# The second convolution of an audio tower as three fp32r products of high and low parts, with a shorter opening and weights loaded later

## What is computed

```python
h = x[:, None, :]                      # x: 64 x 4000
for w, g, b, s in zip(conv_ws, ln_gs, ln_bs, strides):   # (128,10,5), 4 x (128,3,2), 2 x (128,2,2)
    h = _conv1d(h, w, s)
    h = jnp.swapaxes(h, -2, -1)
    h = _fp32_layernorm(h, g, b)       # over the 128 channels
    h = jnp.swapaxes(h, -2, -1)
    h = jax.nn.gelu(h, approximate=False)
h = _fp32_layernorm(jnp.swapaxes(h, 1, 2), fln_g, fln_b) @ proj_w + proj_b    # 64 x 12 x 192
h = h + _L0_attn_ref(_layernorm(h), w_qkv, w_proj, b_proj)    # 12 heads, 64 landmarks, iterated inverse
h = h + _L0_ffn_ref(_layernorm(h), ...)                       # 8 experts, top 2, and a shared one
```

## Time and profile before

| | |
|---|---|
| median of 3 runs | 970.81 us (970.58 to 972.19) |
| the profiled execution | 965.42 us, span 963.7 us |
| PE busy | 711.2 us, 74% of the span, 3435 records |
| DVE busy | 631.7 us, 66%, 1471 instructions |
| ACT busy | 306.4 us, 32%, 505 instructions |
| products of L564, fp32 | 291.7 us, 720 records |
| copies of L724, 128x800 and smaller | 56.6 us, 58 instructions |
| squares of L625 | mean 0.86 us |
| mean granted clock of TensorE | 0.864 of full speed |

### The profile page before, as it was taken

The page is one execution under the profiler, slowest core; times in us unless marked ns, Lnnn a source line. Parts: engine busy times, 40 slices in busy tenths (PEclk is TensorE's granted clock), DMA queues, the critical chain, the costliest instruction groups (busy, mean ns, idle before and its releaser), DMA issues. The chain is left out here.

```text
span 963.7 us, 10716 instructions
## 1 busy us (share of the span) xinstructions
PE 711.2 (74%) x3435; PEld 511.1 (53%) x3435; DVE 631.7 (66%) x1471; ACT 306.4 (32%) x505; POOL 214.2 (22%) x253
## 2 busy tenths in 40 slices
PE   0069998999879997999897536544554446399987
PEld 0026664656545664566564325434554445399977
DVE  4918655774658555144645455899999999734377
ACT  0042345333432344332323121202333321136433
POOL 3000000000000000000000030655776679218401
PEclk9999998999979998899997557767777777879999
DMA  1350420024000410000000070000000000200000
GB/s 56 43 124 1 92 48 1 1 39 101 0 2 0 92 36 0 1 1 1 0 1 1 2 302 0 1 0 0 1 0 0 0 0 0 74 0 1 2 1 25
DMA packets 22553, 25.29 MB, mean 26 GB/s; under 512 B 17052, under 2 KB 21212, under 8 KB 21404
## 3 DMA queue, kind: packets, MB, share of 16 engines
q1 hardware_dynamic: 22508, 24.74, 10.5%
HBM read 21.05 MB, written 3.66 MB: 26 GB/s over the span
## 5 line engine op out<-in xcount | busy, mean ns | idle before, releaser
L564 PE MATMUL ps<-h,w 128*128 128x400 f32 x720 | 291.7, 549 | 1.9 <-ACT h L632 1.8
L564 PEld LDWEIGHTS ps<-h,w 128*128 128x128 f32 x720 | 139.6, 200 | 106.0 <-issue 103.3
L1055 PE MATMUL pt<-for_pe,ident 128*128 128x156 f32 (+2 forms) x420 | 98.4, 415 | 86.1 <-DVE for_pe L1248 86.1
L1055 PEld LDWEIGHTS pt<-for_pe,ident 128*128 128x128 f32 x420 | 90.3, 277 | 94.2 <-DVE for_pe L1248 90.2
L724 DVE COPY h<-ps 128x800 f32<-128x800 f32 (+2 forms) x58 | 56.6, 975 | 95.7 <-PE ps L564 95.0
L577 PEld LDWEIGHTS ps<-averager,sq 128*100 128x100 f32 (+2 forms) x1024 | 100.7, 173 | 22.9 <-ACT sq L625 18.6
L577 PE MATMUL ps<-averager,sq 128*100 128x1 f32 (+2 forms) x1024 | 101.2, 229 | 8.5 <-ACT sq L625 8.1
L625 ACT ACTIVATE sq<-h 128x800 f32<-128x800 f32 (+2 forms) x58 | 49.8, 858 | 177.9 <-DVE h L724 177.9
L632 ACT ACTIVATE h<-h,lnp 128x800 f32<-128x800 f32 (+2 forms) x58 | 60.5, 1042 | 83.1 <-DVE h L755 81.2
L755 DVE TENSOR_TENSOR h<-h,ps 128x400 f32<-128x400 f32 (+2 forms) x116 | 60.0, 559 | 38.2 <-PE ps L593 38.2
L604 ACT ACTIVATE h<-ps,lnp 128x800 f32<-128x800 f32 x64 | 63.4, 1010 | 63.5 <-PE ps L525 63.3
(11 more groups left out here) (268 smaller groups left out, 1032.2 us busy)
## 6 DMA issues: line engine op xcount, KB each, us to landing
late<-windows_dram SPq DMA_DIRECT2D x24, 375.0 KB, 7.4
gate_w<-in_gate_w SPq DMA_DIRECT2D x1, 3456.0 KB, 13.6
up_w<-in_up_w SPq DMA_DIRECT2D x1, 3456.0 KB, 19.1
windows_dram<-parts SPq DMA_DIRECT2D x12, 250.0 KB, 5.0
acts<-in_down_w SPq DMA_DIRECT2D x1, 1728.0 KB, 7.9
w<-in_w SPq DMA_DIRECT2D x1, 1024.0 KB, 6.2
xs<-in_x SPq DMA_DIRECT2D x4, 252.5 KB, 4.2
out_tokens<-hidden SPq DMA_DIRECT2D x6, 96.0 KB, 1.6
```

Source lines behind the costliest of these rows:

```text
L564: mm = pe.matmul(out, w[:, L.first_tap + t, :], source(l, s, 2 * p + c, t), start=(t == 0), stop=(t == L.taps - 1))
L1055: mm = pe.matmul(pt[:, job.bank + n, 0:wide], ident[:, :], sum_buffers[n][:, k * wide:(k + 1) * wide], start=(k == 0), stop=(k == job.term ...
```

## The change

The second convolution's fp32 products become fp32r products of parts. ScalarE rounds each batch of `h0` to fp32r (`rounded`, into `h0_hi`), VectorE takes what is left (`remainder`, into `h0_lo`); both have four places in turn (`TURNS`). The weights of layer 1 are split once. A batch then takes nine products: high by high, low weights by high, high weights by low, three taps each. `h0` is written with even and odd positions apart, so that each product reads 400 positions in a row. A new entry `split` in the plan is the rounding and the remainder of one batch; three of the next round's stand behind `conv(3, 1, 0)`. Round 0 gets a plan of its own: an opening of 3 first products in place of 9, and two instead of one in each of six steps of the section. `attention_weights` moves to the head of `expert_weights`, and the tiles that it fills are allotted there; some tiles of the tower's start share the space of later ones, which adds a wait for `w0_in` on VectorE.

```diff
 AHEAD = GROUP + 1
-POS0, ROW0 = 800, 802
+OPENING = 3
+POS0 = 800
+PLANE = POS0 // 2 + 1
+TURNS = 4
+SPLIT_AHEAD = 3
...
-def round_plan(last):
+def round_plan(last, opening=False):
...
+    waiting = list(range(OPENING if opening else AHEAD, ROUND))
+    soon = lambda: first(waiting.pop(0))
+    split = lambda *batches: [order.append(("split", int(b >= ROUND), b % ROUND // GROUP, b % GROUP)) for b in batches]
+    in_turn = lambda b: lambda: split(b)
+    catch_up = lambda: soon()() if opening else None
     prep(0, 2)
-    conv(1, 0, 0, first(9))
+    catch_up()
+    split(3)
+    conv(1, 0, 0, soon(), in_turn(4))
     prep(2, 4)
-    conv(1, 0, 1, first(10), var(1, 0, 0))
+    catch_up()
+    split(5)
+    conv(1, 0, 1, soon(), in_turn(6), var(1, 0, 0))
...
-    conv(1, 1, 1, first(14), rows(1, 0), var(1, 1, 0), scale(1, 0, 0, 1))
+    catch_up()
+    split(13)
+    conv(1, 1, 1, soon(), in_turn(14), rows(1, 0), var(1, 1, 0), scale(1, 0, 0, 1))
...
-    conv(1, 1, 2, first(15), var(1, 1, 1), scale(1, 0, 4, 5))
+    conv(1, 1, 2, soon(), in_turn(15), var(1, 1, 1), scale(1, 0, 4, 5))
+    assert not waiting
...
+        split(*range(ROUND, ROUND + SPLIT_AHEAD))
...
+    def __init__(self, rounds, per, ahead=AHEAD):
+        self.pair = ahead + per["pair"] * rounds
         self.conv, self.sets = per["conv"] * rounds, per["norm"] * rounds
+        self.split = SPLIT_AHEAD + ROUND * rounds
...
-        h0 = sb("h0", [P, 2, GROUP, ROW0])
+        h0 = sb("h0", [P, 2, GROUP, 2, POS0 // 2])
+        h0_hi, h0_lo = (sb(n, [P, TURNS, 2, PLANE], F32R) for n in ("h0_hi", "h0_lo"))
+        w1_hi, w1_lo = (sb(n, [P, L1.taps, CH], F32R) for n in ("w1_hi", "w1_lo"))
...
-        w0_parts = sb("w0_parts", [K0, PARTS, CH], BF16)
-        w0_rest = sb("w0_rest", [K0, CH])
...
-        w0_pairs = sb("w0_pairs", [P, K0, K0])
...
+        w0_parts = parts[0:K0, 0, :, :].rearrange("p k t -> p (k t)")[:, 0:PARTS * CH].rearrange("p (a c) -> p a c", a=PARTS)
...
+        w0_pairs = flat_u[:, 0:K0 * K0].rearrange("p (a b) -> p a b", a=K0)
+        w0_rest = flat_u[0:K0, K0 * K0:K0 * K0 + CH]
...
-            if batch >= AHEAD:
+            if plan is opening and batch < OPENING:
+                return batch + 1
+            if plan is opening or batch >= AHEAD:
                 return o.pair + number_of(plan, "first", 0, s, b, "pair") + 1
-            if isinstance(r, int) and r == 0:
-                return batch + 1
...
+        def wait_batch_read(eng, plan, r, o, batch):
+            if batch < 0:
+                if isinstance(r, int) and r == 0:
+                    return
+                b = batch + ROUND
+                pair, halves = o.pair - per["pair"] + number_of(body, "conv", 1, 1, b % GROUP // 2, "pair"), ROUND // 2 * (r - 1)
+            else:
+                b = batch
+                pair, halves = o.pair + number_of(plan, "conv", 1, b // GROUP, b % GROUP // 2, "pair"), ROUND // 2 * r
+            if b % 2:
+                eng.wait_ge(y_ready, pair + 1)
+            else:
+                eng.wait_ge(batch_read, halves + b // 2 + 1)
...
-                attention_weights(sp, io, res)
...
+                read_first = OPENING + number_of(opening, "first", 0, 0, GROUP - 1, "pair") + 1
...
-                    sp.wait_ge(y_ready, AHEAD + per["pair"] * (r - 1))
+                    sp.wait_ge(y_ready, max(AHEAD, read_first) + per["pair"] * (r - 1))
...
-                pool.memset(h0[:, :, :, POS0:ROW0], 0.0).then_inc(s_const, 1)
+                pool.memset(h0_hi[:, :, :, PLANE - 1:PLANE].bitcast(F32), 0.0).then_inc(s_const, 1)
+                pool.memset(h0_lo[:, :, :, PLANE - 1:PLANE].bitcast(F32), 0.0).then_inc(s_const, 1)
...
-                for b in range(AHEAD):
-                    if b % GROUP == 0:
-                        pe.wait_ge(win_in[b // GROUP], SLOT_IN)
+                pe.wait_ge(win_in[0], SLOT_IN)
+                for b in range(OPENING):
                     if b >= 2:
                         pe.wait_ge(y_taken, b - 1)
-                    first(b, (b + AHEAD) % 2)
+                    first(b, (b + OPENING) % 2)
...
-                            if l == 1 and p == 0:
-                                pe.wait_ge(win_in[s], SLOT_IN * (r + 2))
+                            if p == 0:
+                                pe.wait_ge(win_in[s], SLOT_IN * (r + l + 1))
...
-                                pe.wait_ge(y_taken, batch_taken(plan, r, o, GROUP * s + 2 * p + c))
+                                pe.wait_ge(lo_done, ROUND * r + GROUP * s + 2 * p + c + 1)
...
-                            for t in range(L.taps):
-                                mm = pe.matmul(out, w[:, L.first_tap + t, :], source(l, s, 2 * p + c, t),
-                                               start=(t == 0), stop=(t == L.taps - 1))
+                            if l == 1:
+                                hi, lo = h0_hi[:, (2 * p + c) % TURNS, :, :], h0_lo[:, (2 * p + c) % TURNS, :, :]
+                                products = [(a, b, t) for a, b in ((w1_hi, hi), (w1_lo, hi), (w1_hi, lo)) for t in range(L.taps)]
+                                for j, (a, b, t) in enumerate(products):
+                                    mm = pe.matmul(ypair[n["bank"]][:, c, 0:L.cols], a[:, t, :], b[:, t % 2, t // 2:t // 2 + L.pos],
+                                                   start=(j == 0), stop=(j == len(products) - 1))
+                                if not c:
+                                    mm.then_inc(batch_read, 1)
...
-                    act.activation(h0[:, s, p, 0:POS0].rearrange("p (h t) -> p h t", h=2), ypair[b][:, :, 0:400],
+                    act.activation(h0[:, s, p, :, :].rearrange("p q (h i) -> p q h i", h=2),
+                                   ypair[b][:, :, 0:POS0 // 2].rearrange("p h (i q) -> p q h i", q=2),
                                    ACT.Gelu, scale=lnp[:, 0:1], bias=lnp[:, 1:2]).then_inc(y_taken, 1)
 
+                def rounded(s, p):
+                    act.copy(h0_hi[:, p % TURNS, :, 0:POS0 // 2], h0[:, s, p, :, :]).then_inc(hi_done, 1)
...
-                for b in range(AHEAD):
-                    first(b // GROUP, b % GROUP, (b + AHEAD) % 2, b)
+                for b in range(OPENING):
+                    first(b // GROUP, b % GROUP, (b + OPENING) % 2, b)
+                for b in range(SPLIT_AHEAD):
+                    act.wait_ge(y_taken, b + 1)
+                    rounded(0, b)
...
+                        elif what == "split":
+                            act.wait_ge(y_taken, batch_taken(plan, r, o, GROUP * s + p, l))
+                            wait_batch_read(act, plan, r, o, ROUND * l + GROUP * s + p - TURNS)
+                            rounded(s, p)
...
-                        if not (isinstance(r, int) and r == 0):
+                        if isinstance(r, int) and r == 0:
+                            dve.wait_ge(w0_in, 16 * PARTS * PARTS)
+                        else:
...
+                dve.wait_ge(s_w0, 5)
...
-                nc.vector.nop(nofuse=True).then_inc(weights_ready, 1)
+                steps.done(nc.vector.tensor_copy(w1_hi[:, :, :], w[:, 0:L1.taps, :]))
+                steps.settle()
+                nc.vector.tensor_tensor(w1_lo[:, :, :], w[:, 0:L1.taps, :], w1_hi[:, :, :].bitcast(F32),
+                                        ALU.subtract).then_inc(weights_ready, 1)
...
+                def remainder(s, p):
+                    nc.vector.tensor_tensor(h0_lo[:, p % TURNS, :, 0:POS0 // 2], h0[:, s, p, :, :],
+                                            h0_hi[:, p % TURNS, :, 0:POS0 // 2].bitcast(F32), ALU.subtract).then_inc(lo_done, 1)
+                for b in range(SPLIT_AHEAD):
+                    dve.wait_ge(hi_done, b + 1)
+                    remainder(0, b)
...
+                        elif what == "split":
+                            dve.wait_ge(hi_done, o.split + n["split"] + 1)
+                            remainder(s, p)
...
-                run(body, 0, Origin(0, per))
+                run(opening, 0, Origin(0, per, OPENING))
...
-    return {"ident": sb("ident", [P, P]), "ident_b": sb("ident_b", [P, P], BF16),
-            "expert_pick": sb("expert_pick", [PICK_ROWS, PICK_TILES, P], BF16), "h6": sb("h6", [P, TOK]), "lnp": sb("lnp", [P, 16]),
-            "proj_w": sb("proj_w", [CH, D]), "qkv_w": sb("qkv_w", [96, KD, 3 * D]),
-            "out_w": sb("out_w", [96, KD, D]),
+    return {"ident": sb("ident", [P, P]), "h6": sb("h6", [P, TOK]), "lnp": sb("lnp", [P, 16]),
...
+    res.update(ident_b=sb("ident_b", [P, P], BF16), expert_pick=sb("expert_pick", [PICK_ROWS, PICK_TILES, P], BF16),
+               proj_w=sb("proj_w", [CH, D]), qkv_w=sb("qkv_w", [96, KD, 3 * D]), out_w=sb("out_w", [96, KD, D]))
...
+            attention_weights(sp, io, res)
```

(20 more changed lines are left out.)

21 lines of the change are left out of this document (15 added, 6 removed).

## The result

The changed kernel takes 1007.62 us (median of 4 runs, 1006.95 to 1008.6) against 971.5 us: 1.0373 times the time before, 95% interval 1.0338 to 1.0407, 36.1 us slower. 997.0 was forecast, 981 to 1015 the range. The profiled execution took 1008.6 us (span 1006.9), 43.2 us more than the profiled one of before; where the 7 us more than between the medians lie is told with e9_loads_alone.

A forecast was written before the change was run, and what follows sets the result against it. TensorE bounds some slots and VectorE others; TensorE alone bounds the last round. Middle rounds +13.8, round 0 +7.5, last round -3.15, loads +1.4, clock +6.4: +26 on the 970.81 median, 997 us, range 981 to 1015.

The forecast's parts named there:

- six tenths of its clock: Lower granted clock from TensorE's idle time: 2.8 in three rounds, 2.2 in the last, 10.6 us; six tenths taken, +6.4.
- the last round's slot 0: Stretch ahead of the last round's first L724 copy, TensorE-bound, partly at the low clock: -1.2 us.
- list of loads: SyncE's issues between tower and attention: three attention-weight issues join them, in the open, +1.4 us; their landing is hidden.
- slot 5: Fifth copy-to-copy time: batch 14 made and split inside, a chain of about 8.0 against 7.25 us, +0.75 in middle rounds.
- Slots 1 and 2: First two copy-to-copy times of a middle round: two remainders each, minus VectorE's idle time, +0.95 us together.
- slot 3: Third copy-to-copy time of a middle round, VectorE having next to no idle time: +1.7 us.
- slot 4: Fourth copy-to-copy time: remainders ahead of the norm, +1.8 us in middle rounds; -0.3 in the last round.
- tail and slot 0: Round's end, three splits ahead of the norm, +1.8 us; then the stretch before the next first copy, +1.05.
- TensorE's gain: A pair of batches takes 18 fp32r records at 0.18, 3.24 us against 4.31: 1.0 us less per TensorE-bound slot.
- Slower, but less: Rival: slots 5 and the tails cost nothing (-14), so +12, 983 us; chance 0.19.
- The clock's rival: Rival: clock stays low through most layer-1 sections, 12 us a round, up to 1036, half of that 1015; chance 0.15.
- Two rivals' sums: Faster, TensorE bounding every slot, 941 us, chance 0.05; fp32r taking fp32's time, 1170 us, chance under 0.01.

The follow-up runs named there:

- e9_loads_alone: Kernel before, with only the seven weight loads that SyncE issued between tower and attention moved into the attention's block: 968.07 us, 0.9951.
- e6_loads: Changed kernel with the whole list of weight loads issued by SyncE inside the attention's own block; split and opening unchanged: 1002.4 us, 1.0306 of the kernel before.
- e3_short_rest: Changed kernel with each remainder cut to 4 elements a partition in place of 800, all products, roundings and waits kept: 978.68 us, 1.0055 of the kernel before.
- e4_split14_later: Changed kernel with the split of batch 14, made within the slot, moved behind that slot's conv: 1003.01 us, 1.0350 of the kernel before.
- e1_fp32: Changed kernel with fp32 products again and no split; short opening, even and odd layout and late loads stay: 977.34 us, 1.0047 of the kernel before.
- e2_pool: Changed kernel with the remainders computed by GpSimd in place of VectorE, everything else the same: 1011.43 us, 1.0415 of the kernel before.
- e5_opening9: Changed kernel with the opening of nine first products taken back from the kernel before: 1011.74 us, 1.0391 of the kernel before.
- e10_even_odd_alone: Kernel before with even and odd positions of h0 apart, fp32 products reading without gaps, but the changed kernel's start kept: 972.09 us, 0.9995.

## Why the prediction was right, and where it was off

The sign, the cause and the size of the main term held; the sum came out 10 us short (26 forecast, 36.1 between medians). The steps, with the profiled executions beside each other; the forecast is put together from the terms of the prediction, each with six tenths of its clock (a middle round 1.7, the last 1.3); the last round's slot 0 (-1.2) lies ahead of its first copy and stands in the third line. How much two executions of one tower can differ shows in the last column, e6_loads (the tower of after) against e9_loads_alone (the tower of before).

| step | forecast | measured | a second pair |
|---|---|---|---|
| to round 1's first copy | +10.2 | 187.41 - 176.43 = +11.0 | 190.19 - 179.01 = +11.2 |
| from there to round 2's | +8.6 | 120.73 - 109.28 = +11.4 | 119.42 - 111.64 = +7.8 |
| from there to the last round's | +6.4 | 116.02 - 108.26 = +7.8 | 118.81 - 110.39 = +8.4 |
| last round, to the tower's last copy | -0.6 | 154.30 - 149.99 = +4.3 | 154.00 - 150.50 = +3.5 |
| list of loads | +1.4 | 16.19 - 12.78 = +3.4 | 8.47 - 8.47 = 0, no list there |
| attention and experts | 0 | +5.3, the luck told above | 410.91 - 411.69 = -0.8 |

Both pairs agree that the forecast of the last round is 4 to 5 us short. In the second line the pairs lie on either side of it, and the first agrees by luck in part, as told under slot 5.

**Right.** The remainders' price: 0.90 us start to start was worked out from the earlier trace rows, and two of them take 1.80 (198.40 to 200.20). VectorE's +58 us came as 58.8. The first copy was put at 68.7 and stands at 68.69. Slots 1 and 2 of round 1 were to cost 0.95 and cost 0.78; slot 3 1.7 and 1.84; slot 4 1.8 and 1.72. The attention's projection waits for no load. e3_short_rest shows that the remainders' length is the main cause, and not only stands beside it: 29 of 36 us.

**Slot 5: the working right, the clock's share mis-sized.** The chain was worked out as 8.0 us, plus a clock price of 1.5 of which six tenths were taken, 0.9 a round. It took 9.84. With the 1.88 us that e4_split14_later measures for the half clock in this slot, the kernel after would have 7.96 at full clock. So the chain's 8.0 stands, the price was 1.9 and not 1.5, and it was paid in full in both middle rounds. In the last round slot 5 takes 9.69 us, +3.65 where +1.95 was forecast. Furthest off is round 0: its slot 5 was put at 8.85 us (+2.8) and takes 12.29 (+6.25), at a granted clock of 0.52 from copy to copy. Timeline of PE, after; the two batches' first products:

```profile
100.44 1.37 PE L615 MATMUL ps<-h_hi,w_hi 128*128 128x400 f32 x3 [3.92 <-DVE h L807]
...
108.18 1.47 PE L615 MATMUL ps<-h_hi,w_hi 128*128 128x400 f32 x3
```

Both batches' nine products lie in the open there, 3.17 us (100.44 to 103.61) and 3.27 (108.18 to 111.45), where nine take 1.71 at full clock (439.70 to 441.41): 3.0 of the 3.4 us missed. The first line of the table comes out nearly right all the same because the way from round 0's eighth copy to round 1's first cost 1.3 us and not the 2.9 of tail and slot 0, and the clock's 1.7 had been set down for the whole round.

For slots 1 and 2, where 0.3 was set down (1.4 of 1.6 leaves 0.2), nothing was paid in round 1, for VectorE covered the half clock; 0.6 in round 2 (a slot of 7.01). The passage of the Trainium skill that I set against my sum ("TensorE: Matmul & The Clock Gate", A second HAM failure mode: psum-queue depth-cycling) would have had all 10.6 us paid, some 4 more: the trace agrees for slot 5 and shows less of it elsewhere.

**The last round: a wait left out.** I took slot 4 as -0.3 and it is +1.48 (8.50 us); I wrote that "copy, square, var and norm make one chain there, and only var starts earlier". The plan puts two remainders ahead of the norm, and the second belongs to a batch made within the slot. ScalarE and DVE of the kernel after:

```profile
444.16 1.01 ACT L661 ACTIVATE h<-ps,lnp 128x800 f32<-128x800 f32 x1
...
445.08 0.85 ACT L666 CAST h_hi<-h 128x800 fp32r<-128x800 f32 x1
...
445.96 0.99 DVE L795 TENSOR_TENSOR h_lo<-h,h_hi 128x800 fp32r<-128x800 f32 x1 [0.68 <-ACT h_hi L666]
...
446.87 0.18 DVE L821 TENSOR_SCALAR vs<-ps 100x32 f32<-100x32 f32 x1
```

Activation, rounding, remainder, and only then the norm (446.87), which could have begun once the variances lay in PSUM near 445.1 (443.56 and 1.57 of L634); no run moves this split, so the 1.7 us are read from this timeline alone. The work on VectorE was costed as nothing here because VectorE was idle; its place in the queue was not.

**TensorE's gain was 0.7 us a slot and not 1.0.** The undisturbed slots of the last round are 5.30 us (436.31 to 441.61), where the kernel before has 6.01. The fp32r records follow each other at 0.19 us (nine from 439.70 to 441.41), where 0.18 was worked out from the earlier trace rows. The rest of the slot grew: from the first product's start to the first conv product it is now 1.91 us (437.79 to 439.70), where it was 1.70 (407.89 to 409.59 in the kernel before). Over 32 slots that is some 9 us of supposed gain that was never there, though only those slots that TensorE bounds felt it, most of them in the last round.

**The list of loads.** The three issues were costed by their own durations (+1.4). The attention begins 3.4 us later, for the issues behind them grew too: the second `router_w` from 0.58 to 2.24 us. How much is a matter of the execution: 2.31 in e1_fp32, but 0.92, 1.14 and 1.20 in e2_pool, e3_short_rest and e5_opening9, which have the same list, so that the attention begins 2.1 us later in these. Why an issue is longer when three more transfers stand in front was not tried.

**Rivals.** "Slower, but less" wanted slot 5 and the tails for nothing: slot 5 alone is +2.59. The clock's rival (1015 to 1036) named the right mechanism; it was paid mainly in one slot a round and not in most. Two rivals' sums don't come out of their terms, which changes no chance: 970.8 - 32 + 1.4 is 940 and not 941, and nine records at 0.359 are 3.2 us a batch against 2.15 for six, 1.1 us more and not 3, some 1040 and not 1170.

## What to carry to other kernels

An engine that is idle for a quarter of a stretch need not have room for work that must be done between two of its queue's fixed points: cost added work slot by slot, and along the queue, also where the engine is idle, since what matters there is who stands behind the wait. Before moving work from VectorE to GpSimd, see what VectorE runs meanwhile: here its instructions with inputs in SBUF waited, and its copies from PSUM didn't. And a list of DMA issues that stands between two blocks costs every engine its length; issued inside the next block nothing waited for it here, and moving it there took some 5 us off both kernels (1.4 to 8.2 on the kernel before).

## What the runs showed of the hardware

- VectorE instructions with two SBUF inputs stood still for a GpSimd instruction with two SBUF inputs: 0.26 us became 1.71. So did a TENSOR_SCALAR with one: 0.17 us became 1.58 (297.49 in e2_pool). Copies from PSUM stayed at 0.98.
- The records of fp32 products, two a product, follow each other at 0.335 us when they read without gaps (405.80 to 407.81, six records in e10_even_odd_alone), and at 0.352 when they read every second position (404.72 to 407.89, nine in the kernel before). That shortened a slot by 0.2 us, and the kernel by nothing that 12 runs could show (0.9995 [0.9966, 1.0023], with a start that was 1 to 2 us later in its profiled execution).
- One tower, unchanged, took 7.6 us more in one profiled execution than in another, with the granted clock below full in more of its slots. A comparison of two single profiles of this kernel can't show less than that; over 23 runs the kernel before spread from 965.3 to 980.8 us.
- The issue of one small DMA on SyncE took 0.54 to 0.58 us where five loads stand ahead of it in its list (three kernels), and 0.92 to 2.31 us where eight do (nine kernels). So what stands ahead of it is not all that decides: the same list has both 0.92 and 2.31.
